# The last stage of a transformer kernel: spare rows written by ScalarE, a fourth buffer of transposed parts, four tiles summed in other PSUM banks

## The chip, the cores and the metric

The kernel runs on one NeuronCore of a Trainium2 chip. The metric is the device time in microseconds of one execution. The median of three runs of the kernel before is 757.25 us, with 757.1 and 757.83 us as the lowest and highest.

## The reference, cut to what matters

The whole is two layers of cross-attention and feed-forward over x of 32 batches x 64 rows x 512, each with a residual sum. The change is in the last of the four parts, a projection with a low-rank term whose weights are mixed over eight experts:

```python
x = x + _L1_ffn_ref(_layernorm(x, axis=-1), W, b, A, Bmat, LiMEs)

def _L1_ffn_ref(x, W, b, A, Bmat, LiMEs):
    H = jnp.einsum('btd,od->bto', x, W) + b
    z = jnp.einsum('btd,dr->btr', x, A)              # rank 32
    ...                                              # gating on rows 1, 3, 5, ...:
    H_slice, delta_slice -> logits -> softmax -> top-2 threshold -> weights
    weights_full = jnp.repeat(weights, 2, axis=1)
    p_mix = jnp.einsum('bte,er->btr', weights_full, LiMEs)
    delta = jnp.einsum('btr,ro->bto', z * p_mix, Bmat) * (16.0 / 32)
    return H + delta
```

The two scales of the gating are maxima over all rows, so no tile can get its delta until all sixteen tiles have given z and the first columns of H.

## The kernel before, in words

x lies in SBUF as 16 tiles of 128 rows x 512 (k.x). The last stage is the function projection_and_experts, one block in which every engine has its own list of instructions, written out by hand; engines meet only at semaphores, and each runs its list in order. The stage before it is query_side; a barrier (shown as L1310 in the rows) lies between the two.

**Feeding.** For each tile i, VectorE (DVE) writes the normed tile x_s (tail_normed, L191; two buffers), ScalarE (ACT) writes its f16 high part into x_n (tail_high, L200), DVE the low part (tail_low, L208), and the queue of SyncE (SP) turns both into x_T with one transposing DMA (tail_turn, L216). Here x_n has three buffers: tile i may be written into x_n[i % 3] only when the DMA of tile i - 3 has landed. Tiles 0 to 2 are made in the stage before (READY = 3).

**TensorE, first part.** For each tile it does twelve matmuls of 40 columns (L1866: z and eight columns of H, from high and low parts), and then four matmuls of 512 columns (L1832) of the "products": the product H for twelve of the sixteen tiles (product_of), twelve matmuls each, used as filling. Now and then come four transposes of z (turn, L1855) or eight small matmuls of z with LiMEs (z_limes, L1846). ACT evicts the products into hb (L1679) and z (L1688 to L1695). GpSimd (POOL) adds each product to its tile of x (add_product, L1646).

**Gating.** DVE works through L1749 to L1791 with two Exp on ACT (L1713, L1717) while TensorE goes on with products, until it transposes the weights (L1889) and multiplies them with LiMEs (L1896).

**Last part.** For q = 0 to 3, DVE writes zp = p_mix * z (scaled, L1803), ACT copies it as f16 into zs (L1683), and POOL subtracts to leave the rest of the f16 rounding in rows 64 to 95 (rest, L1650). Rows 96 to 127 of zs are constant: they carry the bias b and are written once (SELECTED). For each of the 16 tiles in order, one matmul of zs with bm_parts (L1911) gives delta and bias. The four tiles that are not in product_of (10, 14, 11, 15; numbers 10, 11, 14, 15 of the order) have no product yet: their twelve matmuls (L1832) are done here, into the same bank as their L1911. The banks psD[n % 4] go round; DVE adds each to x (result, L1811), and SP stores the tile (L1637).

Of the kernel before, what the change touches and what calls it, by code (L numbers as in the profile page):

```python
# [52 lines left out]
READY = 3  # L53

# [140 lines left out]
def tail_high(act, k, i):  # L195

    tl = k.tl
    act.wait_ge(tl.xs_ok, i + 1)
    wait(act, tl.xT_in[i % 3], 16 * (i // 3))
    act.activation(tl.x_n[i % 3][:, 0, :], tl.x_s[i % 2][:, :], ACT.Copy).then_inc(tl.xhi_ok, 1)  # L200


def tail_low(dve, k, i):

    tl = k.tl
    dve.wait_ge(tl.xhi_ok, i + 1)
    wait(dve, tl.xT_in[i % 3], 16 * (i // 3))
    dve.tensor_tensor(tl.x_n[i % 3][:, 1, :], tl.x_s[i % 2][:, :], tl.x_n[i % 3][:, 0, :], ALU.subtract).then_inc(tl.xlo_ok, 1)  # L208


def tail_turn(sp, k, i):
# [4 lines left out]
    sp.dma_start_transpose(tl.x_T[:, i, :, :], tl.x_n[i % 3][:, :, :].rearrange("p a b -> p (a b)")).then_inc(tl.xT_in[i % 3], 16)  # L216
# [122 lines left out]
def key_side(nc, a, k):  # L339

    with ExitStack() as ctx:
# [35 lines left out]
        CONSTS = 9  # L377
# [149 lines left out]
        def _(dve):  # L527
# [79 lines left out]
            dve.wait_ge(const_ok, len(consts) + 1)  # L607
# [971 lines left out]
def projection_and_experts(nc, a, k):  # L1579
# [9 lines left out]
    SELECTED = 3  # L1589
    MADE = PRODUCTS * 3 * NC  # L1590
    with ExitStack() as ctx:
# [5 lines left out]
        sel = s.sb("sel", [P, 1])  # L1597
# [23 lines left out]
        a_ps, lnk, act_ok, p_ps, zp_ok, zs_ok, z_fin, d_ps, o_ok, wT_ps, wT_ok, done_v = (s.sem(n) for n in (  # L1621
            "a_ps lnk act_ok p_ps zp_ok zs_ok z_fin d_ps o_ok wT_ps wT_ok done_v").split())
# [3 lines left out]
        out = a["out"].rearrange("(t b) d l -> t (b d) l", b=2)  # L1626

# [13 lines left out]
        def _(pool):  # L1641
# [6 lines left out]
            def rest(q):  # L1648
                pool.wait_ge(zs_ok, q + 1)
# [11 lines left out]
            pool.wait_ge(b_ok, SELECTED)  # L1661
# [5 lines left out]
            for q in range(4):  # L1667
                pool.wait_ge(b_ok, SELECTED + FIRST + 2 + q)
# [7 lines left out]
        def _(act):  # L1676
# [20 lines left out]

            act_x(act)
# [326 lines left out]
```

## Time and profile before

| what | value |
|---|---|
| median of three runs | 757.25 us |
| the profiled execution, own time | 760.02 us |
| its span | 758.2 us |
| mean granted TensorE clock | 0.964 |
| PE busy | 683.5 us, 90% |
| DVE busy | 610.3 us, 80% |
| ACT busy | 489.1 us, 65% |
| POOL busy | 383.5 us, 51% |
| last stage | from 682.7 us to the end |

Times in rows are microseconds from the span's start, unless a column says ns. PE is the matmuls of TensorE, PEld its weight loads. The span is the profiled execution without what lies around it (here 1.82 us), and the profiled execution as a whole is 2.77 us above the median of the plain runs. A granted clock of 1.00 is 2.4 GHz, 0.50 is 1.2 GHz.

### The profile page before, as it was taken

The page shows a single profiled execution, that of the slowest core. Times are in us where ns is not written, and L with a number is a line of the kernel's source. Part 1 is how long each engine was busy: PE and PEld are TensorE (multiplying, and loading weights), DVE is VectorE, ACT ScalarE, POOL GpSimd, SP SyncE. Part 2 cuts the span into 40 slices and gives each one's busy share as a digit, 9 for nine tenths or more (in the row PEclk, how much of TensorE's full clock was granted, in tenths as well). Part 3 has the DMA queues.
Part 4 walks back from the last instruction along what each step waited for, and adds up shares of the span by engine and source line. Part 5 has one row for each costly group of instructions (what it writes and reads, how often), then busy time and mean ns, then how long its engine had stood idle before and what let it go on. Part 6 is the DMA issues. An engine that isn't in the chain of part 4 may idle for free. (4 is left out here: it accounts for less than half of the span.)

```text
span 758.2 us, 17720 instructions
## 1 busy us (share of the span) xinstructions
PE 683.5 (90%) x6622; PEld 351.3 (46%) x6649; DVE 610.3 (80%) x971; ACT 489.1 (65%) x884; POOL 383.5 (51%) x331
## 2 busy tenths in 40 slices
PE   6999999999978767599999869999999999958997
PEld 2455445454546555444444324444444444424643
DVE  6878788978745667579999868999999999958355
ACT  3888867676715666577677617878878878754320
POOL 2000009999944676432212317768777687634224
PEclk9999999999998999799999969999999999997899
DMA  5234555556334223014333200000000000025405
GB/s 169 66 127 138 201 183 146 141 155 172 82 83 130 65 68 81 10 35 78 78 69 63 65 19 1 1 2 1 1 2 1 1 2 1 1 42 109 73 1 222
DMA packets 92600, 54.71 MB, mean 72 GB/s; under 512 B 76964, under 2 KB 76964, under 8 KB 92516
## 3 DMA queue, kind: packets, MB, share of 16 engines
q1 hardware_dynamic: 91764, 53.06, 26.7%
q8 instruction: 54, 0.88, 0.5%
q10 hardware_dynamic: 752, 0.52, 0.2%
q14 instruction: 30, 0.25, 0.1%
HBM read 32.00 MB, written 4.19 MB: 48 GB/s over the span
## 5 line engine op out<-in xcount | busy, mean ns | idle before, releaser
L1432 POOL TENSOR_TENSOR query_qn<-query_eq,query_rq 128x1024 f32<-128x1024 f32 x64 | 122.0, 1906 | 53.3 <-DVE query_rq L1366 51.3
L684 ACT ACTIVATE keys_ek<-keys_psK,keys_mk 128x512 f32<-128x512 f32 x128 | 86.9, 684 | 40.0 <-DVE keys_mk L536 38.2
L536 DVE TENSOR_REDUCE keys_mk<-keys_psK 128x2 f32<-128x1024 f32 x64 | 78.0, 1218 | 17.2 <-PE keys_psK L743 16.9
L1357 DVE TENSOR_REDUCE query_mq<-query_psQ 128x16 bf16<-128x1024 f32 x64 | 75.5, 1180 | 4.9 <-PE query_psQ L1520 4.7
L1451 ACT ACTIVATE query_eq<-query_psQ 128x1024 f32<-128x1024 f32 x64 | 65.2, 1019 | 21.5 <-PE query_psQ L1533 21.5
L1363 DVE TENSOR_REDUCE query_lq<-query_eq 128x16 f32<-128x1024 f32 x64 | 77.3, 1207 | 2.2 <-ACT query_eq L1451 2.1
L1542 PE MATMUL query_psX<-all_ident,query_qn 128*128 128x128 f32 x512 | 70.7, 282 | 0.4 <-ACT query_qT L1458 0.4
L754 PE MATMUL keys_psT<-all_ident,keys_ek 128*128 128x128 f32 x512 | 70.8, 282 | 0.0
L766 PE MATMUL keys_psG<-keys_eT,keys_cT 128*64 128x512 f32 x256 | 69.0, 617 | 1.0 <-issue 0.9
L754 PEld LDWEIGHTS keys_psT<-all_ident,keys_ek 128*128 128x128 f32 x512 | 55.5, 142 | 28.2 <-issue 20.0
L1458 ACT ACTIVATE query_qT<-query_psX 128x1024 f32<-128x1024 f32 x64 | 65.4, 1022 | 1.1 <-PE query_psX L1542 1.1
L1182 POOL TENSOR_SCALAR ff_hr<-ff_h,ff_qs 128x1376 f32<-128x1376 f32 x16 | 22.7, 1419 | 81.7 <-DVE ff_qs L1228 78.8
L1542 PEld LDWEIGHTS query_psX<-all_ident,query_qn 128*128 128x128 f32 x512 | 55.5, 142 | 16.3 <-issue 15.5
L1552 PE MATMUL query_psF<-query_qT,all_M 128*64 128x512 f32 x256 | 61.8, 604 | 1.1 <-ACT query_qT L1458 1.1
L501 POOL TENSOR_SCALAR keys_st<-all_ring 128x1024 bf16<-128x1024 f32 (+2 forms) x16 | 60.7, 3796 | 1.3
L489 POOL TENSOR_SCALAR keys_cs_hi<-all_cf 128x512 f16<-128x512 f32 x16 | 10.0, 627 | 97.0 <-DMA all_cf<-in_ctx_dram 86.4
L541 DVE COPY keys_eT<-keys_psT 128x512 f32<-128x512 f32 x80 | 53.2, 681 | 3.0 <-PE keys_psT L754 3.0
L1283 PE MATMUL ff_psG<-all_wgT,all_ff_xT 128*128 128x512 bf16 (+1 forms) x190 | 46.1, 365 | 4.2 <-PEq L857 3.3
L1255 ACT ACTIVATE ff_r<-ff_psG,all_sg 128x512 f32<-128x512 f32 (+1 forms) x48 | 30.9, 643 | 28.1 <-PE ff_psG L1283 26.5
L1288 PE MATMUL ff_psU<-all_wuT,all_ff_xT 128*128 128x512 bf16 (+1 forms) x188 | 45.0, 362 | 0.2
L1832 PE MATMUL tail_psH<-all_ring,all_tl_x_T 128*128 128x512 f16 x168 | 44.5, 409 | 0.3 <-DVE all_x_res L1811 0.3
L1297 PE MATMUL ff_psD<-all_wdT,ff_hT 128*128 128x512 bf16 (+1 forms) x171 | 41.2, 391 | 3.6 <-DMA ff_hT<-ff_hq 3.2
(270 smaller groups left out, 1442.2 us busy)
## 6 DMA issues: line engine op xcount, KB each, us to landing
all_ring<-in_L_ffn_w_down_dram SPq DMA_DIRECT2D x8, 688.0 KB, 4.6
all_ring<-in_L_ffn_w_gate_dram SPq DMA_DIRECT2D x10, 512.0 KB, 5.4
all_ring<-in_L_ffn_w_up_dram SPq DMA_DIRECT2D x10, 512.0 KB, 4.0
all_x_res<-in_x_dram SPq DMA_DIRECT2D x4, 1024.0 KB, 6.2
att_ctx_n<-in_ctx_dram SPq DMA_DIRECT2D x16, 256.0 KB, 3.1
out_dram<-all_x_res SPq DMA_DIRECT2D x16, 256.0 KB, 2.1
all_cf<-in_ctx_dram SPq DMA_DIRECT2D x15, 256.0 KB, 2.7
att_w_nat<-in_L_ffn_W_dram SPq DMA_DIRECT2D x4, 256.0 KB, 4.4
```

The costliest lines, as they stand in the source:

```text
L501: pool.tensor_scalar(st[v % 2][:, 0:w], r, -ROUND, 0.0, ALU.add, ALU.add).then_inc(cast_ok, 1)
L536: dve.tensor_reduce(mk[:, c, :], psK[c % 2][:, :, :], X, ALU.max, negate=True).then_inc(mk_ok, 1)
L684: act.activation(ek[t % 2][b][:, c, :], psK[c % 2][:, b, :], ACT.Exp, bias=mk[:, c, b:b + 1], accum_out=le[t % 2][:, b, c:c + 1]).then_inc ...
L754: mm = pe.transpose(chunk(psT[b], c), chunk(ek[t % 2][b][:, c, :], j), k.ident[:, :])
L766: mm = pe.matmul(psG[HALF[b], :], cT[t % 2][:, j, b * D:(b + 1) * D], eT[b][:, j, :], start=j == 0, stop=j == NC - 1)
L1357: dve.tensor_reduce(mq[g % 2][:, :, 0:HEADS], psQ[g % 2][:, :, :].rearrange("p b (h d) -> p b h d", d=D), X, ALU.max, negate=True).then_in ...
L1363: dve.tensor_reduce(lq[:, :], eq[g % 3][:, :, :], X, ALU.add).then_inc(lq_ok, 1)
L1432: pool.tensor_tensor(qn[m % 2][:, :, :], eq[m % 3][:, :, :], rq[m % 2][:, :].unsqueeze(2).broadcast_to([P, 2 * HEADS, D]), ALU.mult).then_ ...
L1451: act.activation(eq[g % 3][:, :, :].rearrange("p h d -> p (h d)"), psQ[g % 2][:, :, :].rearrange("p b n -> p (b n)"), ACT.Exp).then_inc(eq ...
L1458: act.activation(qT[t % 2][:, :, c * P:(c + 1) * P], psX[:, :, :].rearrange("p b (j n) -> p (b j) n", n=P), ACT.Copy).then_inc(qT_ok, 1)
L1542: mm = pe.transpose(psX[:, b, j * P:(j + 1) * P], qn[g % 2][:, b * HEADS + 2 * j:b * HEADS + 2 * j + 2, :].rearrange("p h d -> p (h d)"), ...
L1552: mm = pe.matmul(psF[HALF[b], :], k.M[:, 2 * t + b, j, :], qT[t % 2][:, b * NC + j, :], start=j == 0, stop=j == NC - 1)
```

## The change

Four edits in the last stage:

1. Rows 96 to 127 of zs are written by one ACT instruction over 32 x 2048 (bias_select, after the eviction of product 5), in place of three POOL instructions at the start of the stage. The factor W_SCALE goes from zs to bm_parts, in an earlier stage: there one POOL tensor_scalar covers 128 rows with a factor per row (row_scale, two small memsets at the start) where it covered 96 rows.
2. x_n has four buffers, and as many semaphores (XBUF = 4); READY stays 3.
3. The four full tiles are summed in the banks of psR, each once DVE has read p_mix from that bank: full(0) after the first four outcomes, full(1) after the next four, full(2) and full(3) ahead of the last four. The other twelve keep psD.
4. DVE does all four of scaled before the first result, and ACT does the first two of its f16 copies before the eviction of product 10, and all of them before that of product 11.

```diff
+XBUF = 4
@@ tail_high, tail_low, tail_turn, and PE's wait: i % 3 becomes i % XBUF, as in
-    wait(act, tl.xT_in[i % 3], 16 * (i // 3))
-    act.activation(tl.x_n[i % 3][:, 0, :], tl.x_s[i % 2][:, :], ACT.Copy).then_inc(tl.xhi_ok, 1)
+    wait(act, tl.xT_in[i % XBUF], 16 * (i // XBUF))
+    act.activation(tl.x_n[i % XBUF][:, 0, :], tl.x_s[i % 2][:, :], ACT.Copy).then_inc(tl.xhi_ok, 1)
@@ later_rows
-        pool.tensor_scalar(bm[0:3 * RANK, :], bm[0:3 * RANK, :], 16.0 / RANK * W_SCALE, None, ALU.mult)...
+        pool.tensor_scalar(bm[:, :], bm[:, :], k.row_scale[:, :], W_SCALE, ALU.mult, ALU.mult)...
@@ projection_and_experts
-    SELECTED = 3
+    SELECTED = 1
+    LAST_FULL = [t for t in order if t not in product_of]
+        def bank_of(n):
+            return psR[:, LAST_FULL.index(order[n]), :] if order[n] in LAST_FULL else psD[n % 4][:, :]
@@ POOL
-            pool.tensor_tensor(sel[bias_rows, :], k.ident[bias_rows, 3 * RANK:3 * RANK + 1],
-                               k.ident[bias_rows, 3 * RANK + 1:3 * RANK + 2], ALU.add).then_inc(b_ok, 1)
-            pool.memset(zs[bias_rows, :, :, :], 1.0).then_inc(b_ok, 1)
-            pool.wait_ge(b_ok, 2)
-            pool.tensor_scalar(zs[bias_rows, :, :, :], zs[bias_rows, :, :, :], sel[bias_rows, :], W_SCALE, ALU.mult,
-                               ALU.mult).then_inc(b_ok, 1)
@@ ACT
+            def bias_select():
+                act.activation(zs[bias_rows, :, :, :].rearrange("p q g n -> p (q g n)"),
+                               k.ident[bias_rows, 3 * RANK:3 * RANK + 1].broadcast_to([RANK, 4 * 4 * P]), ACT.Identity,
+                               bias=k.ident[bias_rows, 3 * RANK + 1:3 * RANK + 2]).then_inc(zs_ok, 1)
...
             turned(3)
             product(5)
+            bias_select()
...
             product(9)
-            product(10)
             scaled(0)
             scaled(1)
-            product(11)
+            product(10)
             scaled(2)
             scaled(3)
+            product(11)
@@ DVE
-            scaled(0)
-            scaled(1)
             for q in range(4):
-                for g in range(4):
-                    result(4 * q + g)
-                    if g == 1 and q < 2:
-                        scaled(q + 2)
+                scaled(q)
+            for m in range(TILES):
+                result(m)
@@ PE
-            for n, t in enumerate(order):
-                bank = psD[n % 4]
-                ...
-                wait(pe, o_ok, n - 3)
-                if t not in product_of:
-                    for m in range(3 * NC):
-                        projected(t, bank, m, False)
+            def full(f):
+                pe.wait_ge(zp_ok, f + 1)
+                for m in range(3 * NC):
+                    projected(LAST_FULL[f], psR[:, f, :], m, False)
+            def outcome(n):
+                ...
+                if t in product_of:
+                    wait(pe, o_ok, n - 3)
                 pe.wait_ge(z_fin, n // 4 + 1)
+                pe.matmul(bank_of(n), zs[:, t % 4, t // 4, :], k.bm_parts[:, :], start=t in product_of,
+                          stop=True).then_inc(d_ps, 1)
+            for q in range(4):
+                if q > 0:
+                    full(q - 1)
+                for n in range(4 * q, 4 * q + 4):
+                    if n == 12:
+                        full(3)
+                    outcome(n)
```

Three places show how instructions move. The first is ACT at the start of the stage, before, from the two small instructions of rstd on: the high parts of tiles 3 to 8 (all_tl_x_n), with the eviction of product 0 (tail_hb) and of z between them. The wait all_tl_xT_in names the buffer whose DMA must have landed.

```order
L120 ACTIVATE all_rs_y<-all_rs_ln 128x8 [waits all_rs_ln_ok]
L200 ACTIVATE all_tl_x_n<-all_tl_x_s 128x512 [waits all_tl_xT_in0,all_tl_xs_ok]
L200 ACTIVATE all_tl_x_n<-all_tl_x_s 128x512 [waits all_tl_xT_in1,all_tl_xs_ok]
L200 ACTIVATE all_tl_x_n<-all_tl_x_s 128x512 [waits all_tl_xT_in2,all_tl_xs_ok]
L200 ACTIVATE all_tl_x_n<-all_tl_x_s 128x512 [waits all_tl_xT_in0,all_tl_xs_ok]
L1679 ACTIVATE tail_hb<-tail_psH 128x512 [waits tail_h_ps]
L200 ACTIVATE all_tl_x_n<-all_tl_x_s 128x512 [waits all_tl_xT_in1,all_tl_xs_ok]
L1688 ACTIVATE tail_raw<-tail_psR 128x32 [waits tail_n_ps]
L1690 ACTIVATE tail_zr<-tail_psR 128x512
```

The same place of ACT in the changed kernel:

```order
L121 ACTIVATE all_rs_y<-all_rs_ln 128x8 [waits all_rs_ln_ok]
L201 ACTIVATE all_tl_x_n<-all_tl_x_s 128x512 [waits all_tl_xs_ok]
L201 ACTIVATE all_tl_x_n<-all_tl_x_s 128x512 [waits all_tl_xT_in0,all_tl_xs_ok]
L201 ACTIVATE all_tl_x_n<-all_tl_x_s 128x512 [waits all_tl_xT_in1,all_tl_xs_ok]
L201 ACTIVATE all_tl_x_n<-all_tl_x_s 128x512 [waits all_tl_xT_in2,all_tl_xs_ok]
L1679 ACTIVATE tail_hb<-tail_psH 128x512 [waits tail_h_ps]
L201 ACTIVATE all_tl_x_n<-all_tl_x_s 128x512 [waits all_tl_xT_in3,all_tl_xs_ok]
```

No instruction changed its place; the fourth of them, tile 6, now waits for the DMA of tile 2, where it waited for that of tile 3.

The second place is the end of ACT's list, before, from the last z copy (tail_zT) on; tail_d2e and tail_d2w are the two Exp of the gating, tail_zs the f16 copies.

```order
L1695 ACTIVATE tail_zT<-tail_psR 128x512 [waits tail_z_ps]
L1679 ACTIVATE tail_hb<-tail_psH 128x512 [waits tail_h_ps]
L1713 ACTIVATE tail_d2e<-tail_d2l 128x128 [waits tail_done_v]
L1679 ACTIVATE tail_hb<-tail_psH 128x512 [waits tail_h_ps] x2
L1717 ACTIVATE tail_d2w<-tail_d2u 128x128 [waits tail_done_v]
L1679 ACTIVATE tail_hb<-tail_psH 128x512 [waits tail_h_ps] x3
L1683 ACTIVATE tail_zs<-tail_zp 96x512 [waits tail_zp_ok] x2
```

And in the changed kernel:

```order
L1679 ACTIVATE tail_hb<-tail_psH 128x512 [waits tail_h_ps]
L1700 ACTIVATE tail_zs<-all_ident 32x2048
L1720 ACTIVATE tail_d2e<-tail_d2l 128x128 [waits tail_done_v]
L1679 ACTIVATE tail_hb<-tail_psH 128x512 [waits tail_h_ps] x2
L1724 ACTIVATE tail_d2w<-tail_d2u 128x128 [waits tail_done_v]
L1679 ACTIVATE tail_hb<-tail_psH 128x512 [waits tail_h_ps] x2
L1683 ACTIVATE tail_zs<-tail_zp 96x512 [waits tail_zp_ok] x2
L1679 ACTIVATE tail_hb<-tail_psH 128x512 [waits tail_h_ps]
L1683 ACTIVATE tail_zs<-tail_zp 96x512 [waits tail_zp_ok] x2
```

The new instruction (L1700) stands ahead of the first Exp, and the first two f16 copies ahead of one eviction that they followed.

The third place is TensorE near the end, before, from the outcome of tile number 8 to that of number 13; numbers 10 and 11 are full tiles.

```order
L1911 MATMUL tail_psA<-all_bm_parts,tail_zs 128x512 [waits tail_z_fin,tail_o_ok]
L1911 MATMUL tail_psH<-all_bm_parts,tail_zs 128x512 [waits tail_z_fin,tail_o_ok]
L1832 MATMUL tail_psH<-all_ring,all_tl_x_T 128x512 [waits tail_o_ok]
L1832 MATMUL tail_psH<-all_ring,all_tl_x_T 128x512 x11
L1911 MATMUL tail_psH<-all_bm_parts,tail_zs 128x512 [waits tail_z_fin]
L1832 MATMUL tail_psB<-all_ring,all_tl_x_T 128x512 [waits tail_o_ok]
L1832 MATMUL tail_psB<-all_ring,all_tl_x_T 128x512 x11
L1911 MATMUL tail_psB<-all_bm_parts,tail_zs 128x512 [waits tail_z_fin]
```

And in the changed kernel, from the first full tile (ahead of number 4) to number 11:

```order
L1836 MATMUL tail_psR<-all_ring,all_tl_x_T 128x512 [waits tail_zp_ok]
L1836 MATMUL tail_psR<-all_ring,all_tl_x_T 128x512 x11
L1919 MATMUL tail_psA<-all_bm_parts,tail_zs 128x512 [waits tail_z_fin,tail_o_ok]
L1919 MATMUL tail_psH<-all_bm_parts,tail_zs 128x512 [waits tail_z_fin,tail_o_ok] x2
L1919 MATMUL tail_psB<-all_bm_parts,tail_zs 128x512 [waits tail_z_fin,tail_o_ok]
L1836 MATMUL tail_psR<-all_ring,all_tl_x_T 128x512 [waits tail_zp_ok]
L1836 MATMUL tail_psR<-all_ring,all_tl_x_T 128x512 x11
L1919 MATMUL tail_psA<-all_bm_parts,tail_zs 128x512 [waits tail_z_fin,tail_o_ok]
```

The full tiles' matmuls stand between groups of four outcomes and wait only for DVE's read of their bank (tail_zp_ok).

## Rows read from the trace of the kernel before

**Rows 1.** Busy time, granted clock (PEclk) and DMA in three stretches.

```profile
687.00:696.00 9.00, 5.77 (x77) 3.02 (x74) 8.10 (x9) 3.27 (x7) 4.56 (x3) 1.00 0.62 118
697.00:707.00 10.00, 9.99 (x75) 6.10 (x75) 7.20 (x11) 5.48 (x11) 2.43 (x2) 0.50 0.77 118
707.00:737.00 30.00, 30.00 (x235) 16.79 (x233) 12.57 (x50) 9.22 (x19) 6.10 (x5) 1.00 0.14 27
```

**Rows 2.** Timeline of PE, tiles 5 and 6: start, duration; [idle before <- releaser].

```profile
691.76 0.47 PE L1866 MATMUL tail_psR<-all_ring,all_tl_x_T 128*128 128x40 f16 x12 [1.13 <-DMA all_tl_x_T<-all_tl_x_n]
...
695.64 0.47 PE L1866 MATMUL tail_psR<-all_ring,all_tl_x_T 128*128 128x40 f16 x12 [2.10 <-DMA all_tl_x_T<-all_tl_x_n]
```

**Rows 3.** The chain that ended last, 699 to 709 us: start, duration.

```profile
699.31 1.80 PE tail_psA L1846 x8
...
701.63 1.71 PE tail_psH L1832 x4
...
708.09 0.87 PE tail_psH L1832 x4
708.96 0.98 PE tail_psA L1846 x8
```

**Rows 4.** SP's queue, tiles 3 and 4, and 5; then issues of 682 to 758 us.

```profile
684.81 2.61 SPq L216 DMA_TRANSPOSE all_tl_x_T<-all_tl_x_n  x2
...
688.66 1.23 SPq L216 DMA_TRANSPOSE all_tl_x_T<-all_tl_x_n  x1
...
all_tl_x_T<-all_tl_x_n SPq DMA_TRANSPOSE x13, 3.2
```

**Rows 5.** Timeline of POOL at the start of the stage.

```profile
685.91 1.80 POOL L1657 MEMSET tail_zs<- 32x2048 f16 x1
687.82 2.53 POOL L1659 TENSOR_SCALAR tail_zs<-tail_zs,tail_sel 32x2048 f16<-32x2048 f16 x1
```

**Rows 6.** Timeline of DVE in the same stretch.

```profile
684.77 0.55 DVE L191 TENSOR_SCALAR all_tl_x_s<-all_x_res,all_mv,all_rstd 128x512 f32<-128x512 f32 x1
...
685.95 2.04 DVE L191 TENSOR_SCALAR all_tl_x_s<-all_x_res,all_mv,all_rstd 128x512 f32<-128x512 f32 x1
...
688.63 2.01 DVE L191 TENSOR_SCALAR all_tl_x_s<-all_x_res,all_mv,all_rstd 128x512 f32<-128x512 f32 x1
```

**Rows 7.** Timeline of ACT: the high part of tile 6, and the first Exp.

```profile
688.10 0.63 ACT L200 ACTIVATE all_tl_x_n<-all_tl_x_s 128x512 f16<-128x512 f32 x1 [2.13 <-DMA all_tl_x_T<-all_tl_x_n]
...
723.09 0.31 ACT L1713 ACTIVATE tail_d2e<-tail_d2l 128x128 f32<-128x128 f32 x1 [2.97 <-DVEq L1772]
```

**Rows 8.** The page's costliest groups: busy us, mean ns of one.

```profile
L1458 ACT ACTIVATE query_qT<-query_psX 128x1024 f32<-128x1024 f32 x64 | 65.4, 1022 | 1.1 <-PE query_psX L1542 1.1
```

**Rows 9.** Timelines of DVE (the weights done) and PE (their transposes).

```profile
728.71 0.29 DVE L1791 TENSOR_TENSOR tail_wf<-tail_d2w,tail_r 128x128 f32<-128x128 f32 x1
...
730.24 0.60 PE L1889 MATMUL tail_psB<-all_ident,tail_wf 128*128 128x128 f32 x4
```

**Rows 10.** Waits from 736 us: total, times, longest; then PE's first full tile.

```profile
PE tail_psA L1911 <- POOL tail_zs L1650: 2.4, 2, 1.3
...
743.25 2.76 PE L1832 MATMUL tail_psH<-all_ring,all_tl_x_T 128*128 128x512 f16 x12 [0.28 <-DVE all_x_res L1811]
```

**Rows 11.** Timelines of DVE and POOL: the first two scaled, the first two rests.

```profile
733.09 1.29 DVE L1803 TENSOR_TENSOR tail_zp<-tail_psR,tail_zT 128x512 f32<-128x512 f32 x2 [1.33 <-PE tail_psR L1896]
...
735.93 1.15 POOL L1650 TENSOR_TENSOR tail_zs<-tail_zp,tail_zs 32x512 f16<-32x512 f32 x1 [4.30 <-ACT tail_zs L1683]
...
738.51 1.15 POOL L1650 TENSOR_TENSOR tail_zs<-tail_zp,tail_zs 32x512 f16<-32x512 f32 x1
```

**Rows 12.** The end: timeline of PE and DVE, then landing of the stores.

```profile
737.23 0.38 PE L1911 MATMUL tail_psA<-all_bm_parts,tail_zs 128*128 128x512 f16 x1
...
755.12 0.69 DVE L1811 SCALAR_TENSOR_TENSOR all_x_res<-tail_psB,all_x_res 128x512 f32<-128x512 f32 x1 [2.12 <-PE tail_psB L1911]
...
DMA to landing us min/median/max: 2.0/2.1/3.0
```

More of the change, by code:

```diff
@@ L206, in tail_low @@
     dve.wait_ge(tl.xhi_ok, i + 1)
-    wait(dve, tl.xT_in[i % 3], 16 * (i // 3))
-    dve.tensor_tensor(tl.x_n[i % 3][:, 1, :], tl.x_s[i % 2][:, :], tl.x_n[i % 3][:, 0, :], ALU.subtract).then_inc(tl.xlo_ok, 1)
+    wait(dve, tl.xT_in[i % XBUF], 16 * (i // XBUF))
+    dve.tensor_tensor(tl.x_n[i % XBUF][:, 1, :], tl.x_s[i % 2][:, :], tl.x_n[i % XBUF][:, 0, :], ALU.subtract).then_inc(tl.xlo_ok, 1)
 def tail_turn(sp, k, i):
@@ L301, in later_rows @@
         pool.wait_ge(k.b_in, 16 * (2 + k.n_late - k.n_weights))
-        pool.tensor_scalar(bm[0:3 * RANK, :], bm[0:3 * RANK, :], 16.0 / RANK * W_SCALE, None, ALU.mult).then_inc(row_ok, 1)
+        pool.tensor_scalar(bm[:, :], bm[:, :], k.row_scale[:, :], W_SCALE, ALU.mult, ALU.mult).then_inc(row_ok, 1)
         pool.wait_ge(row_ok, 1)
@@ L606, in _ @@
             dve.memset(k.wabs[:, :, :], 0.0).then_inc(const_ok, 1)
-            dve.wait_ge(const_ok, len(consts) + 1)
+            dve.memset(k.row_scale[0:3 * RANK, :], 16.0 / RANK).then_inc(const_ok, 1)
+            dve.memset(k.row_scale[3 * RANK:P, :], 1.0).then_inc(const_ok, 1)
+            dve.wait_ge(const_ok, len(consts) + 3)
             for h in range(2):
@@ L1620, in projection_and_experts @@
             "z_ps z_ok n_ps zr_ok h_ps hb_ok b_ok").split())
[L1621 to L1622 removed]
+        a_ps, lnk, act_ok, zp_ok, zs_ok, z_fin, d_ps, o_ok, wT_ok, done_v = (s.sem(n) for n in (
+            "a_ps lnk act_ok zp_ok zs_ok z_fin d_ps o_ok wT_ok done_v").split())
         store = k.store
@@ L1898, in _ @@
                                wT[r0:r0 + EXPERTS, t // 4, :], start=True, stop=True)
-            mm.then_inc(p_ps, 1)
+            mm.then_inc(a_ps, 1)
             products(125, MADE)
-            pe.wait_ge(b_ok, SELECTED)
-            for n, t in enumerate(order):
-                bank = psD[n % 4]
+            pe.wait_ge(zs_ok, SELECTED)
+            def full(f):
[3 more added lines that the diff above has]
+            def outcome(n):
+                t = order[n]
                 if n in (1, 2):
                     pe.wait_ge(hb_ok, PRODUCTS - 2 + n)
-                wait(pe, o_ok, n - 3)
-                if t not in product_of:
-                    for m in range(3 * NC):
-                        projected(t, bank, m, False)
+                if t in product_of:
+                    wait(pe, o_ok, n - 3)
                 pe.wait_ge(z_fin, n // 4 + 1)
-                pe.matmul(bank[:, :], zs[:, t % 4, t // 4, :], k.bm_parts[:, :], start=t in product_of,
+                pe.matmul(bank_of(n), zs[:, t % 4, t // 4, :], k.bm_parts[:, :], start=t in product_of,
                           stop=True).then_inc(d_ps, 1)
+            for q in range(4):
[5 more added lines that the diff above has]
+                    outcome(n)
 def program(nc, a):
@@ L1934, in program @@
         k.m_minus = s.sb("m_minus", [P, 1])
+        k.row_scale = s.sb("row_scale", [P, 1])
         k.half_ln = s.sb("half_ln", [P, 1])
@@ L1992, in program @@
             tl.x_s = [m.sb(f"tl_x_s{p}", [P, L]) for p in range(2)]
-            tl.x_n = [m.sb(f"tl_x_n{i}", [P, 2, L], F16) for i in range(READY)]
+            tl.x_n = [m.sb(f"tl_x_n{i}", [P, 2, L], F16) for i in range(XBUF)]
             tl.x_T = m.sb("tl_x_T", [P, TILES, 2 * NC, P], F16)
             tl.xs_ok, tl.xhi_ok, tl.xlo_ok = (s.sem("tl_" + n) for n in ("xs_ok", "xhi_ok", "xlo_ok"))
-            tl.xT_in = [s.sem(f"tl_xT_in{i}") for i in range(READY)]
+            tl.xT_in = [s.sem(f"tl_xT_in{i}") for i in range(XBUF)]
             query_side(nc, a, k)
```

22 lines of the change are left out of this document (10 added, 12 removed).

## The prediction

> **What bounds the kernel now.** I read the page first: TensorE is busy for 90% of the span, so in most stretches only its idle time, its clock or its work can give time back. The chain that ended last, followed back through the last stage, stays on PE nearly throughout, with one step on a transposing DMA near the start and a knot of POOL, DVE and PE near the end. So I looked at these two places.
>
> At the start the windows show two stretches, with a third behind them [rows 1]. From 687 to 696 us the clock is full, but PE is busy for only 5.77 of 9 us. From 697 to 707 us it is busy for 9.99 of 10 us, at 0.50, which is 1.2 GHz. The idle time has two pieces, 1.13 and 2.10 us, both ended by the DMA of the transposed parts [rows 2]. In the chain, four fills of 512 columns take 1.71 us at the low clock and 0.87 at the full, and eight small matmuls 1.80 against 0.98 [rows 3]. So late tiles cost twice: 3.2 us of idle time, and a low clock after it.
>
> Why are tiles 5 and 6 late? The DMA of tile 5 is issued at 688.66, and 3.2 us pass to the landing, so that of tile 6 was issued at 692.4; the two before, back to back, take 2.61 us of the queue, 1.3 each [rows 4]. Two things hold them back. Ahead of tile 5's low part, DVE writes x_s of tile 6, which takes 2.04 us where tile 4's took 0.55 (I name tiles by their place in DVE's list); one more like it takes 2.01 us at 688.63 [rows 6]. These lie over POOL's memset of 1.80 and tensor_scalar of 2.53 us, 685.91 to 690.35, which write the constant rows of zs [rows 5]. And tile 6's high part waits for a buffer: ACT was idle for 2.13 us until 688.10, when tile 3's DMA landed [rows 7]. DVE passes through tile 7's x_s before the low part of tile 6, so both delays add up.
>
> **Constant rows off POOL, fourth buffer (first gain).** Without POOL's work, and with tile 6 waiting for tile 2, I place the tiles anew. Per tile DVE needs some 1.2 us (x_s 0.55, the low part about 0.7 by my estimate from the gaps between its rows). Tile 5's low part is ready at 687.2 instead of 688.6; its issue follows tile 4's at 684.81 + 2.61 = 687.4, and it lands at 690.6, just as PE has done tile 4's fill, in place of 691.76. Tile 6's high part then comes at 686.5, its low part by 688.4, its issue by 688.7, its landing at 691.9, before PE wants it at 692.3 (PE needs about 1.2 us a tile at full clock, 0.87 of fill and 0.3 of small matmuls, and 0.4 to 1.0 for each of the z steps between). From there the queue can issue each 1.3 us, 10 more tiles in 13 us, so tile 15 lands about 705 at the latest; PE at full clock gets to it at 692.3 + 9 x 1.2 + 2.8 for the z steps, 705.9, and with what follows about 707. What stays late is tile 7 or so: one POOL add of a product (1.3 us) meets DVE there. I charge 1.2 us of idle time left, from a range of 0 to 2.5 (nothing, or two such meetings). Gain on idle time: 3.2 - 1.2 = 2.0 us.
>
> **The clock (second gain).** The low clock follows a stretch with PE busy for 5.77 of 9 us [rows 1]. With idle pieces of well under a microsecond that stretch is nearly full, and the clock should stay at 2.4 GHz. The price of the ten microseconds: between 697 and 707 us there are nearly four fills, each 1.71 - 0.87 = 0.84 dearer, so 3.2; the eight small matmuls, 0.8 [rows 3]; and some 0.5 for transposes and forty-column matmuls. Sum 4.5 us; the bounds are 0 (the clock falls all the same) and 5.0 (everything at half speed).
>
> Does what is won arrive at the end? From 707 to 737 us PE is busy for the whole of the 30 us and at full clock [rows 1]. The gating on DVE starts when tile 15 is through PE, so it moves along with it. It is done at 728.71 + 0.29 = 729.0, PE takes the weights at 730.24 [rows 9], so 1.2 us of slack stay as they are. I count the gain in full.
>
> **The new ACT instruction.** 32 x 2048 elements: 1024 a partition take 1.02 us [rows 8], so 2048 take 1.9 to 2.0. It stands where ACT is idle for 2.97 us ahead of the first Exp [rows 7], so it costs nothing; it would cost something beyond 2.97 + 1.2 = 4.2 us. Queued behind it are the Exp and through it DVE's gating. Bounds: 1.0 and 2.53 us, what POOL took for as many elements [rows 5]; neither reaches 4.2. The f16 factor per row in the earlier stage replaces one POOL instruction by one like it, and the two memsets are of one column; I put them at nothing, hidden behind the loads of the start, at most 0.1 us.
>
> **The last part (third gain).** PE begins the outcomes at 737.23, the last result begins at 755.12 [rows 12]. PE's own work there is 48 matmuls in four full tiles and 16 outcomes: a full tile takes 2.6 us up to its outcome (743.25 to 745.85 on its row, which gives 2.76 with its drain [rows 10]), so 10.4, and the outcomes, at a twelfth of it each, 16 x 0.22 = 3.5, 13.9 us in all, against 17.6. The difference is waiting: 2.4 us in two waits for POOL's rests and the remainder for results that free a bank [rows 10]. In the new order, POOL's first rest can start 1.4 us sooner, since ACT's copies needn't follow the eviction of product 10 (DVE's first scaled ends at 733.7, a copy of 512 elements takes some 0.6 by half of ACT's row for 1024 and a start, so 734.5 instead of 735.93 [rows 8, 11]); the rests then end at about 735.6, 738.2, 740.8 and 743.3, with a period of 2.58 us [rows 11]. PE wants them at 737.2, 741.0, 744.4 and 750.5, a full tile of 2.6 us lying before each group but the first. All are ready. One short wait of 0.3 us for the eviction of product 11 stays. So PE ends near 751.4. The four last results, 0.6 us apart, begin at 750.8, and the last begins at 752.6 instead of 755.12: 2.5 us. But four stores of 256 KB now fall together; landings run from 2.0 to 3.0 us [rows 12], and I charge 0.3 of it, between 0 and 0.9. Gain: 2.2 us, between 1.6 and 2.5.
>
> **The sum.** 2.0 + 4.5 + 2.2 = 8.7 us. Against the profiled execution's own time of 760.02 that is 751.3, against its span of 758.2 it is 749.5. The profiled execution lies 2.77 us above the median of 757.25, so for plain runs I predict 757.25 - 8.7 = 748.5.
>
> A rule that concerns the meetings left over: DVE's 2.04 us beside POOL's 1.80 [rows 5, 6] looks like waiting out the other's instruction. The Trainium skill (SBUF — State Buffer, section SBUF: two separate sides) says that the pair of ports is locked by whichever comes first and the other blocks until it is done. By that, each of three or four POOL adds before the last tile costs DVE up to 1.3 us. By the rule the idle time left would be at the far end of my range, 2.5 us, and the sum 7.4 instead of 8.7.
>
> **The rivals.**
> *A: the clock falls anyway.* The tiles come sooner, but a few short idle pieces remain and some stretch near 690 to 697 us is judged quiet. For it speaks that the fall came about 1.4 us after the last idle piece, so it isn't known which piece did it; against it that idle time shrinks from 3.2 to about 1.2 us. Time: 757.25 - 2.0 - 2.2 = 753.0. The Trainium skill (TensorE: Matmul & The Clock Gate, section A second HAM failure mode) states that short idle pieces between groups can make the clock oscillate, which would lead here.
> *B: only the end gains.* The transposing DMAs limit the feed by themselves: 3.2 us each [rows 4], in one queue. Against it: two are issued back to back in 2.61 us. Time: 757.25 - 2.2 = 755.0.
> *C: only the start gains.* POOL's rests or DVE's sixteen results (0.6 us each, 9.6 in sum) hold the end in another way. Time: 757.25 - 6.5 = 750.7.
> *D: slower.* The low clock comes later and lasts longer: PE now runs ahead of its feed through the stage, and a quiet stretch after 700 us keeps the clock at 0.50 through the gating. Each microsecond of old work there costs about one more. The gains without the clock are 4.2 us, and the old ten low microseconds are worth 4.5, so it decides once some 9 us of work that ran at full clock run at half; 14 us of such work give 757.25 - 8.7 + 14 = 762.5. Nothing in the profile makes such a stretch likely: PE has work throughout from 707 to 737 us [rows 1].
> *E: nothing that can be measured.* The parts cancel: 757.
>
> **How the numbers follow.** Forecast 0.66 (own range 746.5 to 751.2), A 0.14, B 0.06, C 0.06, D 0.04, E 0.04. C lies inside the forecast's range. The range 746.0 to 753.5 holds the forecast and A, and C; its low end takes no idle time left (another 1.2), a dearer clock (0.5), and stores without queueing (0.3), 746.5, and half a microsecond for the four fills at low clock before 687 us. What a measurement tells from no change is about 0.2%, 1.5 us. Faster: 0.92; same: 0.04; slower: 0.04.
>
> **What would show it.** The changed kernel's windows should read 1.00 for the clock from 687 us to the end, and PE's waits for the DMA of the transposed parts under 1.5 us in all; DVE's x_s of tiles 6 and 7 should be at 0.55 us; PE should take tile 15 near 707. The new ACT instruction should take 2 us and be followed by an Exp that waits for DVE, not DVE for it. From the first outcome to the last result's start, 15.4 us instead of 17.9, with no wait of PE for POOL. The prediction is wrong if the clock falls to 0.50 again after 690 us, if PE waits for DMAs as before, or if the last four results are held by POOL's adds.

## The result and the profile after

Over nine runs the changed kernel has a median of 752.95 us (749.89 to 755.36); the kernel before, in nine runs with it, 758.13 us (756.37 to 761.3). The ratio is 0.9928, with a 95% interval of 0.9909 to 0.9947: faster by 0.7%, some 5.2 us by the medians and 4.0 to 6.9 us by the interval. The forecast of 748.5 lies below the fastest run; its range of 746.0 to 753.5 holds the median. In the profiled execution the gain was 8.2 us: span 750.0 us, own time 751.84, mean clock 0.972. So the two profiled executions stand apart by nearly what was forecast (8.7), and the medians by less. The experiments are mostly about that difference. In the comparisons below, two executions of the kernel before that took 889.36 and 891.67 us are counted in its median but left out of the ratio.

The windows of the changed kernel answer to [rows 1]. The columns are the stretch and its length, then the busy time of PE, PEld, DVE, ACT and POOL with the count of instructions, and last the granted clock, the DMA engines' busy share and GB/s:

```profile
687.00:696.00 9.00, 8.64 (x105) 4.50 (x103) 8.52 (x13) 5.99 (x13) 2.61 (x2) 1.00 0.96 184
697.00:707.00 10.00, 9.30 (x122) 6.07 (x119) 5.35 (x9) 4.24 (x9) 2.53 (x2) 1.00 1.00 158
707.00:731.00 24.00, 24.00 (x161) 12.80 (x158) 12.43 (x48) 10.40 (x18) 6.15 (x5) 1.00 0.01 1
```

PE is busy for 8.64 of the 9 us in which it had 5.77, and the clock stays at 1.00. Its timeline, tile 5, tile 6, tile 10 and tile 15 (each the first of the forty-column matmuls), answers to [rows 2]:

```profile
691.45 0.47 PE L1870 MATMUL tail_psR<-all_ring,all_tl_x_T 128*128 128x40 f16 x12
...
693.06 0.46 PE L1870 MATMUL tail_psR<-all_ring,all_tl_x_T 128*128 128x40 f16 x12
...
700.39 0.47 PE L1870 MATMUL tail_psR<-all_ring,all_tl_x_T 128*128 128x40 f16 x12 [0.70 <-DMA all_tl_x_T<-all_tl_x_n]
...
707.76 0.46 PE L1870 MATMUL tail_psR<-all_ring,all_tl_x_T 128*128 128x40 f16 x12
```

One idle piece of 0.70 us is left. The stage began at 683.28 here, so tile 15 comes 24.5 us after the first matmul; the forecast had 707 - 682.7 = 24.3, and before it was 31.1. DVE's timeline answers to [rows 6]:

```profile
686.51 0.55 DVE L192 TENSOR_SCALAR all_tl_x_s<-all_x_res,all_mv,all_rstd 128x512 f32<-128x512 f32 x1
...
687.70 0.55 DVE L192 TENSOR_SCALAR all_tl_x_s<-all_x_res,all_mv,all_rstd 128x512 f32<-128x512 f32 x1
...
689.69 1.48 DVE L209 TENSOR_TENSOR all_tl_x_n<-all_tl_x_s,all_tl_x_n 128x512 f16<-128x512 f32 x1 [0.20 <-ACT all_tl_x_n L201]
```

The x_s of tiles 6 and 7 take 0.55 us each. The idle piece ahead of tile 10 has its cause in that tile's DMA. SP's queue shows the issues for tiles 10 and 11, and the list of DMA issues from 695.7 to 697 us has the time from issue to landing of tile 10's:

```profile
695.72 1.23 SPq L217 DMA_TRANSPOSE all_tl_x_T<-all_tl_x_n  x1
...
697.05 2.27 SPq L217 DMA_TRANSPOSE all_tl_x_T<-all_tl_x_n  x1
...
all_tl_x_T<-all_tl_x_n SPq DMA_TRANSPOSE x1, 4.6
```

Tile 10's DMA was issued at 695.72 and landed 4.6 us later, where those of tiles 3 to 9 took 3.1 to 3.3. The issue of 2.27 us that follows (the others take 1.23 to 1.3) carries tile 11, which PE took at 701.56 without waiting. ACT's timeline, for the new instruction and [rows 7]'s Exp:

```profile
714.08 2.00 ACT L1700 ACTIVATE tail_zs<-all_ident 32x2048 f16<-32x2048 f32 x1
717.03 0.31 ACT L1720 ACTIVATE tail_d2e<-tail_d2l 128x128 f32<-128x128 f32 x1 [0.95 <-DVEq L1779]
```

It took 2.00 us, and ACT still waited 0.95 us for DVE behind it. The end, PE first and then DVE, answers to [rows 10, 12]:

```profile
731.00 0.38 PE L1919 MATMUL tail_psA<-all_bm_parts,tail_zs 128*128 128x512 f16 x1
731.22 0.38 PE L1919 MATMUL tail_psH<-all_bm_parts,tail_zs 128*128 128x512 f16 x1
731.86 0.39 PE L1919 MATMUL tail_psH<-all_bm_parts,tail_zs 128*128 128x512 f16 x1 [0.26 <-ACT tail_hb L1679]
...
744.39 0.38 PE L1919 MATMUL tail_psA<-all_bm_parts,tail_zs 128*128 128x512 f16 x1
```

```profile
738.83 0.69 DVE L1818 SCALAR_TENSOR_TENSOR all_x_res<-tail_psA,all_x_res 128x512 f32<-128x512 f32 x1 [0.97 <-POOL all_x_res L1653]
...
746.08 1.28 DVE L1818 SCALAR_TENSOR_TENSOR all_x_res<-tail_psR,all_x_res 128x512 f32<-128x512 f32 x2
```

PE waits once, 0.26 us, for the eviction of product 11. From the first outcome to the end of the last result there are 747.36 - 731.00 = 16.36 us, where the kernel before has 755.81 - 737.23 = 18.58. DVE waits 0.97 us for a POOL add at the ninth result, which nothing behind it needs in time.

### The profile page after: what moved, and what is told of

It reads as the page before. It is cut to its first block and busy times, and to the rows that moved or that the text cites. A ratio compares the mean times of both kernels' runs of the same rounds, so it can differ in the third digit from the quotient of the medians.

```text
span 750.0 us, 17745 instructions
## 1 busy us (share of the span) xinstructions
PE 678.8 (91%) x6649; PEld 347.7 (46%) x6649; DVE 607.0 (81%) x973; ACT 490.1 (65%) x885; POOL 377.2 (50%) x328
## 3 DMA queue, kind: packets, MB, share of 16 engines
q1 hardware_dynamic: 91764, 53.06, 28.1%
## 5 line engine op out<-in xcount | busy, mean ns | idle before, releaser
L1258 ACT ACTIVATE ff_r<-ff_psG,all_sg 128x512 f32<-128x512 f32 (+1 forms) x48 | 30.8, 643 | 29.5 <-PE ff_psG L1286 27.9
L715 ACT ACTIVATE keys_eT<-keys_psT 128x512 f32<-128x512 f32 x48 | 28.7, 597 | 19.5 <-PE keys_psT L757 19.3
```

## The experiments

The ratios given with the medians are taken over the executions of both kernels and are not the ratios of the medians: the medians of e1_end_only and of its before stand 1.5 us apart, and their means, 757.13 and 757.11, do not.

Each trace was cut at the same four places, read from the timelines: the stage's first forty-column matmul, that of tile 15, the first outcome (the first matmul of zs with bm_parts), and the end of the last result. All traces of this case together, in us:

```
kernel           stage   first to  tile 15 to     first outcome   last result
                 starts  tile 15   first outcome  to last result  to span's end
before           682.72  31.11     23.40          18.58           2.39
e3_before_a      680.52  28.80     23.40          18.57           2.41
e3_before_b      680.97  29.77     23.41          18.57           2.38
e3_before_c      680.01  28.52     23.41          19.59           2.47
e1_buf_only      682.77  29.55     23.41          20.03           2.44
e2_warm          680.54  28.09     23.40          18.58           2.39
e1_end_only      682.04  28.30     23.24          16.36           2.66
e2_end_again     682.81  28.82     23.24          16.36           2.67
e1_bias_only     682.65  25.97     23.40          18.58           2.40
e1_feed_only     682.65  24.32     23.40          18.58           2.45
e3_feed_again    682.56  24.21     23.41          18.57           2.45
changed          683.28  24.48     23.24          16.36           2.64
e2_after_again   683.38  24.51     23.24          16.35           2.72
e2_pair          683.70  24.43     23.24          15.52           2.51
```

**e1_end_only: the last part alone.** The changed kernel with three buffers and POOL's constant rows put back:

```diff
-XBUF = 4
+XBUF = 3
...
+            pool.tensor_tensor(sel[bias_rows, :], k.ident[bias_rows, 3 * RANK:3 * RANK + 1],
+                               k.ident[bias_rows, 3 * RANK + 1:3 * RANK + 2], ALU.add).then_inc(b_ok, 1)
+            pool.memset(zs[bias_rows, :, :, :], 1.0).then_inc(b_ok, 1)
...
-            bias_select()
```

> The new order of the last part alone (edits 3 and 4), with POOL writing the constant rows and three buffers as before. Theory 1 (the parts add up as forecast, and the shortfall of the whole against 8.7 us is the clock's share, which isn't there in each execution): 2.2 us faster than before, between 1.6 and 2.5, with PE's first outcome to the last result's start at 15.2 us instead of 17.9. Theory 2 (the end gains less in plain runs than in the profiled one, since it collides with stores): under 1 us faster.

Median 758.27 (12 runs) against 756.74 (35 runs of before), ratio 1.0002, interval 0.9978 to 1.0026. In its trace the last part takes 16.36 us, 2.2 less than before, as forecast. So the trace has the gain and the plain runs haven't; the expected 0.9971 lies just outside the interval. Four of the twelve runs took 753.9 to 754.4 us, the traced one (754.42) among them, and the other eight 756.9 and more, so the trace shows one of the shorter ones. And the trace showed something more: with the same late tiles as before (idle pieces of 1.09 and 2.06 us), tile 15 came at 28.30 us, not 31.11. Its window, and that of before over the same stretch:

```profile
695.00:710.00 15.00, 14.99 (x167) 9.03 (x167) 8.74 (x14) 8.60 (x17) 3.83 (x3) 0.89 0.85 148
```

```profile
695.00:710.00 15.00, 14.36 (x121) 8.66 (x122) 9.52 (x15) 8.32 (x16) 2.89 (x3) 0.66 0.84 142
```

A mean clock of 0.89 over 15 us makes 3.3 us at 0.50, and 0.66 makes 10.2 us.

**e1_feed_only, e1_bias_only, e1_buf_only: the start, together and apart.** All three start from the kernel before. The first has edits 1 and 2; the second only edit 1; the third only edit 2 (and, to have a semaphore free for the fourth buffer, two waits of DVE moved to another one, as in the changed kernel):

```diff
(bias_only: edit 1 as in the diff of the change, the waits counted accordingly)
-            pool.memset(zs[bias_rows, :, :, :], 1.0).then_inc(b_ok, 1)
...
             product(5)
+            bias_select()
(buf_only)
+XBUF = 4
-    wait(act, tl.xT_in[i % 3], 16 * (i // 3))
+    wait(act, tl.xT_in[i % XBUF], 16 * (i // XBUF))
...
(feed_only: both)
```

> The constant rows on ACT and the fourth buffer (edits 1 and 2), the last part in its old order. Theory 1: the rest of the whole's gain, 3 to 3.5 us in the median, more (6 us) in an execution in which the kernel before has its low clock from 697 to 707 us; its trace shows no idle piece over 0.8 us and a clock of 1.00 from 687 us on. Theory 2: 4.5 us or more in the median.

Median 755.05 (12 runs), ratio 0.9977, interval 0.9948 to 1.0007; the trace has tile 15 at 24.32 us, a clock of 1.00 from 687 us and idle pieces of 0.23 and 0.46 us. The trace is as expected; the gain of the plain runs, 1.7 us, is under the 3 to 3.5 of the first theory, which the interval (up to 3.9) still holds.

> Only the constant rows moved from POOL to ACT, three buffers. Tile 6's high part still waits for tile 3's DMA until 688.1 us, its low part is ready at about 688.8 and its DMA lands at 692.1, before PE wants it. Theory 1: this edit alone gives nearly all of what both give (within 1 us of it), since the two x_s of 2 us are gone. Rival (the buffers are the bound): less than half of it.

Median 755.73 (12 runs), ratio 0.9986, interval 0.9965 to 1.0007. Tile 15 at 25.97 us: in the traces, this edit brings 5.1 of the 6.8 us that both bring against the first trace, 2.6 against the shortest of before. With three buffers ACT still waits for DMAs, here at tile 6 and tile 9:

```profile
688.04 0.63 ACT L200 ACTIVATE all_tl_x_n<-all_tl_x_s 128x512 f16<-128x512 f32 x1 [2.14 <-DMA all_tl_x_T<-all_tl_x_n]
...
692.59 0.63 ACT L200 ACTIVATE all_tl_x_n<-all_tl_x_s 128x512 f16<-128x512 f32 x1 [1.08 <-DMA all_tl_x_T<-all_tl_x_n]
```

PE had one idle piece of 0.85 us and a clock of 0.89 from 695 to 710 us. "Within 1 us" of both was too much: 1.7 us are left for the buffer.

> Only the fourth buffer (and, to have a semaphore free, the two that tell DVE of the weights' transposes and of the sixteen small products counted on a_ps, as in the changed kernel). POOL's memset and tensor_scalar still hold DVE's two x_s for 2 us each. Theory 1: tile 5 and tile 6 stay late (DVE's low part of tile 6 can't come before 691 us), little gain, 0 to 1.5 us, and the clock falls as before. Rival: as much as both.

Median 757.51 (12 runs), ratio 1.0002, interval 0.9981 to 1.0024. As expected, nothing: DVE's two long x_s are there, and tiles 5 and 6 are as late as before.

```profile
686.01 2.04 DVE L192 TENSOR_SCALAR all_tl_x_s<-all_x_res,all_mv,all_rstd 128x512 f32<-128x512 f32 x1
...
688.68 2.01 DVE L192 TENSOR_SCALAR all_tl_x_s<-all_x_res,all_mv,all_rstd 128x512 f32<-128x512 f32 x1
```

By these single traces the fourth buffer is worth 1.7 us behind the other edit, with some 3 us of low clock in the trace that lacks it, and nothing alone: 29.55 us to tile 15 is also the mean of before's four traces.

**e2_warm: idle time or something else behind the low clock.** The kernel before, with work that nobody reads in the two idle pieces:

```diff
             for i in range(TILES):
                 hi, lo = parts_of(i)
+                for _ in range({5: 5, 6: 10}.get(i, 0)):
+                    pe.matmul(psB[:, :], x_T[:, 0, 0, :], k.WT_hi[:, 0, :], start=True, stop=True)
                 pe.wait_ge(xT_in[i % 3], 16 * (i // 3) + 16)
```

> The kernel before with 5 matmuls of 512 columns into an unused PSUM bank (results never read) put ahead of tile 5 and 10 ahead of tile 6, so that TensorE works through the two pieces of idle time (1.1 and 2.1 us) while the DMAs are as late as before. If idle time brings the low clock: clock 1.00 from 687 us to the last part, and tile 15 at 26.2 to 27.0 us after the first matmul, where before has 31.1 and the end-only kernel 28.3; its median 1 to 4 us under that of before. If the low clock has another cause, it stays, and tile 15 comes at 28 us or later.

Median 756.91 (12 runs) against 757.86 (27 runs of before), ratio 0.9992, interval 0.9973 to 1.0012. The low clock is gone:

```profile
687.00:695.00 8.00, 7.94 (x77) 3.98 (x76) 6.76 (x9) 3.19 (x8) 2.80 (x3) 1.00 0.62 120
695.00:710.00 15.00, 13.91 (x171) 9.21 (x167) 9.24 (x14) 8.47 (x18) 4.03 (x4) 1.00 0.72 130
```

But tile 15 comes at 28.09 us, not at 26.2 to 27.0, and the median's gain stays under the 1 to 4 us expected. From tile 6 to tile 15 PE takes 15.16 us here and 18.19 in the first trace, so with the old feed ten microseconds of low clock cost 3.0 us and not 4.5. PE at full clock waits for DMAs again, at tiles 10 and 11:

```profile
700.50 0.47 PE L1868 MATMUL tail_psR<-all_ring,all_tl_x_T 128*128 128x40 f16 x12 [0.51 <-DMA all_tl_x_T<-all_tl_x_n]
...
702.42 0.47 PE L1868 MATMUL tail_psR<-all_ring,all_tl_x_T 128*128 128x40 f16 x12 [0.58 <-DMA all_tl_x_T<-all_tl_x_n]
```

Two things hold tile 10 back here. ACT could write its high part only at 694.83, when the DMA of tile 7 had landed; with a fourth buffer it would not have waited for that one. And the issue of its own DMA took 2.09 us, which also puts off that of tile 11.

One trace without a low clock doesn't show yet that filling the idle time did it, since e3_before_c below lacks it too. All traces together say more: of the seven with both idle pieces six have a low clock behind tile 6, and of the six in which they are filled (e2_warm) or are gone (those with edits 1 and 2) none has; e1_bias_only, with one piece of 0.85 us, has 3.4 us of it. So the idle time does bring the low clock, though not each time. And up to some 3 us of low clock cost little, 0 to 0.7 us between the traces at 28.1 to 28.8 us: what PE would win at full speed it waits for at the next tiles. Only a low clock that lasts longer comes on top.

**e2_end_again and e2_after_again, beside it on the same chip.**

> Edits 3 and 4 alone once more, as its trace gained 2.15 us in the last part and its median nothing. Theory C: the last part again 16.4 us from first outcome to last result in the trace, tile 15 between 28 and 31.5 us after the first matmul, by how long the low clock lasts, and the median now 1 to 3 us under before. Rival: the median again equals that of before, so that something outside the last part takes the gain back; then the stretches ahead of the last stage would have to be longer than in before by 2 us.

Median 756.25 (12 runs), ratio 0.9983, interval 0.9962 to 1.0003. The trace repeats 16.36 us. This is within the 1 to 3 us expected, and its interval holds the 2.2 us of the traces, which that of e1_end_only just fails to hold. Its rival asked for stretches ahead of the last stage that are longer than in before: the stage starts at 682.04 and 682.81 us in the two traces of this kernel, 1.4 us later on the mean than in before's four, though one of these, at 682.72, is as late. See what stays open below.

> The changed kernel once more, beside the other three. Theory C (the clock's share varies from one execution to the next, the other shares don't): its trace has tile 15 at 24.0 to 24.9 us after the stage's first matmul, no low clock between 687 and 745 us, and 16.4 us from the first outcome to the end of the last result; its median is 4 to 6 us under that of before.

Median 751.96 (10 runs), ratio 0.993, interval 0.9907 to 0.9953. All segments repeat within 0.1 us; the whole gain is 5.3 us by the ratio.

**e3_before_a, b and c: the kernel before, three more traces.**

> The kernel before itself, for its trace. Theory C (the late tiles are in each execution, the length of the low clock behind them isn't): again 1.1 and 2.1 us of idle time ahead of tiles 5 and 6, 18.6 us from first outcome to the end of the last result, and a low clock of 0 to 10 us behind tile 6, so that tile 15 comes at 27 to 31.2 us after the first matmul, shorter than the 31.11 of the first trace in at least one of these three. Rival: the low clock lasts 10 us each time, and the shortfall of the whole gain (5 us measured against 8.7 forecast) lies elsewhere.

> The kernel before, a second execution, with the same expectation as the first of the three: idle pieces as before, tile 15 at 27 to 31.2 us after the first matmul by the length of the low clock.

> The kernel before, a third execution, with the same expectation as the first of the three: idle pieces as before, tile 15 at 27 to 31.2 us after the first matmul by the length of the low clock.

Single times of 755.52, 756.94 and 755.74 us. Tile 15 comes at 28.80, 29.77 and 28.52 us, all shorter than the first trace's 31.11. The windows from 695 to 710 us, a, b and c in turn:

```profile
695.00:710.00 15.00, 14.54 (x168) 9.13 (x166) 7.88 (x13) 7.89 (x16) 3.46 (x3) 0.91 0.77 129
```

```profile
695.00:710.00 15.00, 14.87 (x151) 9.42 (x150) 8.90 (x14) 7.33 (x16) 3.83 (x3) 0.77 0.82 135
```

```profile
695.00:710.00 15.00, 13.58 (x161) 9.01 (x159) 8.83 (x14) 8.05 (x18) 3.62 (x4) 1.00 0.72 125
```

The idle pieces ahead of tiles 5 and 6 are there each time (1.13 and 2.08 in a, 1.12 and 2.12 in b, 0.67 and 2.13 in c). The low clock behind them isn't of one length: 10 us in the first trace, then 3.5, 7 and none. In c, where it stays away, PE waits at tiles 10 and 11 instead, 0.75 and 0.67 us, as in e2_warm; here too an issue was long, that of tile 10 with 2.55 us. The expectation held in all three. And c has a low clock elsewhere, behind the waits of the last part; its first full tile takes 3.79 us instead of 2.76:

```profile
737.09 0.58 PE L1911 MATMUL tail_psA<-all_bm_parts,tail_zs 128*128 128x512 f16 x1 [1.13 <-POOL tail_zs L1650]
737.47 0.63 PE L1911 MATMUL tail_psH<-all_bm_parts,tail_zs 128*128 128x512 f16 x1
737.95 3.79 PE L1832 MATMUL tail_psH<-all_ring,all_tl_x_T 128*128 128x512 f16 x12
```

**e3_feed_again.**

> Edits 1 and 2 alone once more. Theory C: tile 15 again at 24.2 to 24.7 us in the trace with no low clock after 687 us; the old last part again 18.6 us, or up to 1.5 us more where the clock falls in its waits; median 2 to 4.5 us under before.

Median 753.35 (12 runs) against 757.75 (16 runs), ratio 0.9959, interval 0.9938 to 0.9981. The segments repeat. The medians gain 4.4 us this time and gained 1.7 in e1_feed_only, on another chip; by the ratios it is 3.1 and 1.7. So a gain read from the medians of two such rounds can differ by 2.7 us for one and the same edit.

**e2_pair: a better order at the end.**

```diff
-                    if n == 12:
+                    if n == 14:
                         full(3)
```

> The changed kernel with full(3) put after the outcomes of numbers 12 and 13, so that two results and two stores fall together at the end, not four. The last result then starts 1.2 us sooner after TensorE's last matmul; TensorE's work is the same. Theory: from the first outcome to the end of the last result 15.2 us instead of 16.4, and 2.4 us from there to the end of the span instead of 2.64: 1.4 us faster than the changed kernel by the trace, which the medians may hardly tell. Rival: the result is held by something else, 16.4 us as before.

Median 751.38 (6 runs) against 757.86 (27), ratio 0.991, interval 0.9877 to 0.9943: the fastest version here, though its median can't be told from the changed kernel's. By the trace it is 0.84 us shorter up to the last result and 0.1 to 0.2 behind it. PE's last full tile and DVE's last results:

```profile
742.60 2.75 PE L1836 MATMUL tail_psR<-all_ring,all_tl_x_T 128*128 128x512 f16 x12
745.19 0.59 PE L1919 MATMUL tail_psR<-all_bm_parts,tail_zs 128*128 128x512 f16 x2
```

```profile
743.26 0.68 DVE L1818 SCALAR_TENSOR_TENSOR all_x_res<-tail_psH,all_x_res 128x512 f32<-128x512 f32 x1
745.60 1.29 DVE L1818 SCALAR_TENSOR_TENSOR all_x_res<-tail_psR,all_x_res 128x512 f32<-128x512 f32 x2 [1.66 <-PE tail_psR L1919]
```

Expected were 15.2 us, measured 15.52: I had left out that two outcomes of 0.22 us now stand ahead of the last full tile and push it back by 0.43.

## Why the prediction was right in its mechanisms and too large in its sum

The median of 752.95 lies within the whole range, 746.0 to 753.5, but above the forecast's own, 746.5 to 751.2. The upper end had been set to take in rival A, which is not what happened, so that the whole range held is in part luck.

**What bounds the kernel.** Right at both places. Moving POOL's two instructions away turned the x_s of 2.04 and 2.01 us into 0.55 (after, feed_only), and with only a buffer they stay (buf_only). The late tiles, and the idle pieces of 1.1 and 2.1 us, are there in all four traces of before.

**Constant rows and fourth buffer, 2.0 us.** Placed right: tile 15 at 24.5 us after the first matmul against 24.3 forecast, in five traces 24.2 to 24.5. The idle time left was 0.70 us in one piece, with several gaps of about 0.1 between tiles, against 1.2 charged. The piece that was left, ahead of tile 10, came from that tile's slow DMA and not, as the prediction had it, from a meeting of DVE with POOL near tile 7; in three other traces with both edits tile 7 is late too, by 0.2 to 0.3 us. The meetings with POOL's adds did come, three of them, with DVE instructions of 1.48, 1.48 and 1.34 us where they take 0.55 or 0.69; so each costs DVE 0.7 to 0.9 us, within the "up to 1.3" of the prediction's sum by the rule, and the queue's lead hides most of it. The Trainium skill (SBUF — State Buffer, section SBUF: two separate sides) says that whichever comes first has the ports that DVE and POOL share for its whole instruction, and the other is blocked. The trace agrees: each of the three began 0.1 to 0.5 us after an add of POOL's (1.26 to 1.34 us) and ended 0.3 to 0.6 us after that add's end, so DVE waited for what was left of it. The second of them, DVE's x_s of tile 11 and POOL's add:

```profile
693.50 1.27 POOL L1653 TENSOR_TENSOR all_x_res<-all_x_res,tail_hb 128x512 f32<-128x512 f32 x1 [2.88 <-ACT tail_hb L1679]
```

```profile
693.57 1.48 DVE L192 TENSOR_SCALAR all_tl_x_s<-all_x_res,all_mv,all_rstd 128x512 f32<-128x512 f32 x1
```

**The clock, 4.5 us.** This is the term that was mis-sized. Its mechanism holds: with PE kept busy the clock stays (e2_warm), and no trace with both of the first two edits has a low clock between 688 us and the last part. But the ten microseconds were those of one execution. In four traces of before the low clock behind tile 6 lasts 10, 3.5, 7 and 0 us, and the first 3 or so of them cost little, since a PE at full speed waits at tiles 10 and 11 (e2_warm and e3_before_c). Start and clock together were forecast at 6.5 us; on the mean of before's four traces, 29.55 us to tile 15, they bring 29.55 - 24.5 = 5.05 us. Sizing the clock's part against one trace, and as if PE's speed alone set the time there, overstated it by 1.5 us. Against that one trace the forecast fits, 31.11 - 24.48 = 6.63 us, since with the new feed a PE at full speed also has less to wait for: it takes 14.70 us from tile 6 to tile 15, where e2_warm takes 15.16. But the sum was then taken off the median of the plain runs, which lies 2.77 us below this execution.

**Does it arrive at the end?** Yes: tile 15 to the first outcome is 23.40 us in every trace with the old last part, whatever came ahead of it.

**The ACT instruction, nothing.** Right: 2.00 us in idle time of 2.95.

**The last part, 2.2 us.** Right in the trace: 18.58 - 16.36 is 2.22, some 0.3 of it are given back to the four stores at the end (2.64 to 2.72 against 2.39 to 2.47), as charged, and another 0.16 is gained before the first outcome. That makes 2.1 of the 2.2 forecast; the part ahead of the stores was forecast at 2.5, but the first of the last four results starts 13.9 us after the first outcome, where 750.8 - 737.2 = 13.6 was reckoned. Not foreseen: in two of the nine traces with the old order (e3_before_c, e1_buf_only) a low clock followed its waits, for 1.0 and 1.45 us more. In the new order PE has no such waits, and none of its five traces has a low clock there; five are too few to call the waits its cause.

**The remainder.** In the stage itself, the mean of before's four traces is 74.2 us from first matmul to the span's end, and that of the changed kernel's two is 66.8: 7.4 us. The medians say 5.2. The other 2 us lie ahead of the stage: it starts at 681.1 on the mean in the four traces of before and at 683.3 in those of the changed kernel. The forecast put all that is ahead of the stage at nothing, so this, and not the clock, is the larger part of what is missing. Whether the change causes it isn't shown. The six traces with edit 1 start between 682.6 and 683.7 us, the eight without it between 680.0 and 682.8, so three of those without it start later than the earliest with it. The difference is there by the first matmul of the stage before, at 441.2 to 443.5 us without the edit and 443.2 to 444.2 with it. Part of it is spread between executions: at the last ACT instruction of the feed-forward part (L1258 before), 1.7 of the 2.3 us between the changed kernel and before are there already (428.4 against 426.7 on the mean), while the three traces with edit 1 but the old last part stand at 426.7 to 426.8. These three lose their time behind it, in a stretch with waits and changes of the clock: 16.5 us from there to the next stage's first matmul, against 14.4 to 16.5 without the edit. A version with edit 1's one early instruction alone wasn't run, and the question stays open. So does the smaller gain of the last part alone in plain runs, 0 and 1.3 us by the two ratios where its traces show 2.2 up to the last result.

Of the rivals, A (the clock falls anyway, 753.0) has the time that came out, but not its mechanism: the clock did not fall in the changed kernel; it often falls less in the one before. B, C and D are out by the table of segments, and E by the interval of the result.

## What to carry to other kernels

The length of a low clock behind idle time belongs to one execution; take several traces of the kernel before until its spread is known, price only what lies above the bound that the next engine sets, and take the sum off the same execution that it was read from. A cheap instruction on a slow engine can be dear to its neighbour: look at what runs beside it, not at its own slack. Where engines wait for each other in turn near the end, put the long work that needs nothing of them between the groups that do, and let as few results as possible follow the last matmul.

## What the runs showed of the hardware that wasn't expected

POOL's tensor_scalar over 96 rows took longer than the one over 128 rows that replaced it, for the same 512 elements a row; before and after:

```profile
L302 POOL TENSOR_SCALAR att_bm<-att_bm x1: 1494/1494/1494, 299.3 to 299.3; 96x512 f32<-96x512 f32 x1
```

```profile
L303 POOL TENSOR_SCALAR att_bm<-att_bm,all_row_scale x1: 691/691/691, 299.1 to 299.1; 128x512 f32<-128x512 f32 x1
```

All eight traces without edit 1 have 1.49 or 1.50 us and all six with it 0.69, with the same instructions of DVE beside it in each. The second takes a factor per row and two multiplications, so rows and form changed together, and the cause wasn't taken apart.

The transposing DMA of tile 10 takes longer than its neighbours: 3.5 to 4.9 us from issue to landing in thirteen of the fourteen traces (3.2 in e1_buf_only), where those of tiles 7 to 9 take 3.0 to 3.4. It is the same tile whether it is issued 12 or 16 us after the stage's first matmul; why isn't known, and in the changed kernel it makes the one idle piece that PE has left.

And the runs of one kernel spread over 8 us here (753.11 to 761.55 for the runs of before that are compared), so that differences under 2 us had to be read from segments of traces, not from medians.
